# Narrow heads: the larger of two halves' maxima taken on GpSimd, tile by tile, in place of a reduction on VectorE

## The reference

```python
x = layernorm(x + L0_attn(x))   # causal, 16 heads of dimension 8
x = layernorm(x + L0_ffn(x))    # 8 experts, top 2, relu
x = layernorm(x + L1_attn(x))   # causal, low-rank q and k, 16 heads of dimension 8
x = layernorm(x + L1_ffn(x))    # attention, then 8 experts
```

```python
scores = jnp.einsum('bhsk,bhtk->bhst', Q[..., :KPH], K) / math.sqrt(KPH)
attn = jax.nn.softmax(scores, axis=-1)
ao = jnp.einsum('bhst,bhtv->bhsv', attn, V)
```

## Time and profile before

| | us |
|---|---|
| median of 3 runs | 1165.69 |
| the profiled execution, its own time | 1166.3 |
| its span, first to last instruction | 1164.6 |
| TensorE (PE) busy | 1077.7 (93%) |
| VectorE (DVE) busy | 883.9 (76%) |
| ScalarE (ACT) busy | 764.9 (66%) |
| GpSimd (POOL) busy | 305.0 (26%) |
| reductions L1027, 768 in all | 495.5 |

### The profile page before, as it was taken

How to read it: one execution, slowest core, us unless ns; L and a number is a source line. 1 busy time by engine, 2 the same in 40 slices (tenths; PEclk the granted TensorE clock), 3 DMA queues, 4 the chain that set the end, 5 groups by cost and what they waited for, 6 DMA issues and landing times. The chain is left out here.

```text
span 1164.6 us, 24392 instructions
## 1 busy us (share of the span) xinstructions
PE 1077.7 (93%) x8338; PEld 569.1 (49%) x8338; DVE 883.9 (76%) x2563; ACT 764.9 (66%) x1527; POOL 305.0 (26%) x843
## 2 busy tenths in 40 slices
PE   8999999989999988999999998898889898899997
PEld 5465665656767655666655532221122221137775
DVE  6999989882433497889978899799999899804435
ACT  4576776766444446777776677888888688875443
POOL 4234433231115225433346211230110100100001
PEclk9899999999999999999999999999999999999999
DMA  7355431100001601344222221002111000000000
GB/s 200 75 121 156 104 84 33 43 23 2 1 1 38 157 22 33 96 106 103 66 75 56 55 38 25 18 18 45 26 36 38 11 18 13 6 1 1 10 10 19
DMA packets 39563, 57.62 MB, mean 49 GB/s; under 512 B 9408, under 2 KB 14992, under 8 KB 39056
## 3 DMA queue, kind: packets, MB, share of 16 engines
q1 hardware_dynamic: 39440, 56.06, 19.6%
HBM read 30.81 MB, written 24.64 MB: 48 GB/s over the span
## 5 line engine op out<-in xcount | busy, mean ns | idle before, releaser
L911 ACT ACTIVATE probs<-bank 128x512 f32<-128x512 f32 x1088 | 575.9, 601 | 214.8 <-PE bank L1346 213.6
L1027 DVE TENSOR_REDUCE tile_max<-bank 128x1 f32<-128x512 f32 x768 | 495.5, 683 | 55.6 <-PE bank L1332 53.2
L1332 PE MATMUL bank<-qk 125*128 125x512 bf16 (+1 forms) x1280 | 387.2, 356 | 54.9 <-DVE tile_max L1027 41.3
L1346 PE MATMUL bank<-qk 128*128 128x128 bf16 (+1 forms) x1664 | 384.6, 309 | 5.9 <-ACT probs L911 5.5
L1375 PE MATMUL bank<-probs,v_head 128*32 128x512 f32 (+3 forms) x3328 | 304.1, 454 | 0.1
L1332 PEld LDWEIGHTS bank<-qk 125*128 125x128 bf16 (+1 forms) x1280 | 105.4, 96 | 333.1 <-DVE tile_max L1027 225.4
L1023 DVE CUSTOM_DVE_ANT_0 bank<-bank,future 128x512 f32<-128x512 f32 (+3 forms) x512 | 243.5, 506 | 22.2 <-PE bank L1332 22.1
L1187 DVE SCALAR_TENSOR_TENSOR acc<-bank,gate,acc 128x128 f32<-128x128 f32 x248 | 69.7, 343 | 158.4 <-PE bank L1501 158.4
L1346 PEld LDWEIGHTS bank<-qk 128*128 128x128 bf16 (+1 forms) x1664 | 138.2, 97 | 68.1 <-ACT probs L911 22.0
L1375 PEld LDWEIGHTS bank<-probs,v_head 128*32 128x32 f32 x3328 | 139.7, 109 | 53.4 <-issue 30.5
L931 ACT ACTIVATE probs<-bank,sb_b 128x512 f32<-128x512 f32 x128 | 81.0, 684 | 123.1 <-PE bank L1489 123.1
(11 more groups left out here) (148 smaller groups left out, 648.9 us busy)
## 6 DMA issues: line engine op xcount, KB each, us to landing
qk<-qk_parts SPq DMA_DIRECT2D x160, 144.0 KB
qk_parts<-q_parts SPq DMA_DIRECT2D x48, 192.0 KB, 2.4
qk_parts<-k_parts SPq DMA_DIRECT2D x48, 192.0 KB, 2.9
qk_parts<-q_parts SPq DMA_DIRECT2D x24, 96.0 KB, 2.3
qk_parts<-k_parts SPq DMA_DIRECT2D x24, 96.0 KB, 2.9
sb_w<-in_w SPq DMA_DIRECT2D x8, 256.0 KB, 3.7
sb_w<-in_w SPq DMA_DIRECT2D x2, 1024.0 KB, 5.9
qk<-neg_rows SPq DMA_DIRECT2D x96, 6.0 KB
```

The lines of the kernel that those rows point to most:

```text
L911: nc.scalar.activation(probs[:, hd.probs_place(c), :], S2[i % len(S2)][:], ACT.Exp, scale=hd.a.scale).then_inc(sem("probs"), 1)
L1027: ins = nc.vector.tensor_reduce(largest, s1[:, at:at + P * count], AX.X, ALU.max)
L1332: ins = mm(s1[:, at:at + P * count], qk[hd.query_rows, hd.place, 0, P * t:P * (t + 1)], qk[hd.query_rows, hd.place, 1, P * k0:P * (k0 + co ...
L1346: ins = mm(s2[:, at:at + P * count], qk[hd.key_rows, hd.place, 1, P * j:P * (j + 1)], qk[hd.key_rows, hd.place, 0, P * q0:P * (q0 + count) ...
```

## The change

For the narrow heads alone, the seventeenth instruction on VectorE (L1033, with the wait for its own last reduction) goes. GpSimd waits for the last reduction of the head itself (`max_taken`), and before its four steps runs eight instructions, one for each query tile: the larger of the tile's two columns, times -1, written to one column of `neg_max`. Each has one column as its input, the other as a scalar read from SBUF, and a constant. The eight don't wait for each other; the last one is waited for before the first cast. Where VectorE reuses a slot whose last tenant was a narrow head, it waits for the four steps of that head (`neg_parts`) in place of `neg_max`. Causal heads stay as they are.

```diff
@@ split_max, on GpSimd
                 ge(pool, "neg_ps", g - RING + 1)
-                pool.wait_ge(sem("neg_max"), g + 1)
+                if HEADS[g].a.causal:
+                    pool.wait_ge(sem("neg_max"), g + 1)
+                else:
+                    pool.wait_ge(sem("max_taken"), CHUNKS[g + 1])
+                    for t in range(TB):
+                        ins = nc.gpsimd.tensor_scalar(neg_max[:, slot, t:t + 1], tile_max[:, slot, t, 0:1],
+                                                      tile_max[:, slot, t, 1:2], -1.0, ALU.max, ALU.mult)
+                    link(ins)
                 nc.gpsimd.tensor_copy(neg_parts[:, slot, 0, :], whole_m).then_inc(sem("neg_parts"), 1)
@@ find_max, on VectorE
                 if c == 0:
-                    ge(dve, "neg_max", g - RING + 1)
+                    if g - RING >= 2 * NH:
+                        dve.wait_ge(sem("neg_parts"), 4 * (g - RING + 1))
+                    else:
+                        ge(dve, "neg_max", g - RING + 1)
...
-                if c == a.chunks - 1:
+                if a.causal and c == a.chunks - 1:
                     dve.wait_ge(sem("max_taken"), CHUNKS[g + 1])
                     ge(dve, "neg_parts", 4 * (g - RING + 1))
                     nc.vector.tensor_reduce(neg_max[:, hd.slot, :], tile_max[:, hd.slot], AX.X, ALU.max,
                                             negate=True).then_inc(sem("neg_max"), 1)
```

## The result

The changed kernel takes 1229.74 us, the median of 4 runs (1227.06 to 1230.61), against 1165.35 before (the median of four; the prediction started from 1165.69, that of the first three). The ratio is 1.0545, with a 95% interval of 1.0523 to 1.0568: slower by 64 us. The profiled execution took 1227.06, its span is 1225.3 us against 1164.6, so the spans differ by a little less, 60.8 us, than the medians.

What follows compares the result with a forecast made beforehand. A ring of waits between TensorE and VectorE, with the transposition inside, sets the narrow heads' pace. Shift less cover, 32.3 us, less 0.6 for VectorE gives +31.7: 1197.4 us from 1165.7, range 1172 to 1232.

Steps and rivals of the forecast that it cites:

- rival (1): The forecast itself: GpSimd starts 0.13 to 0.30 us apart, split 1.0 to 2.3 us later, +15 to +56 us; 64%.
- rival (2): GpSimd's instructions dearer, starts 0.30 to 0.45 us apart, +56 to +94 us, or TensorE's clock falls after waits; 16%.
- VectorE's relief: Removing the seventeenth reduction frees 0.20 us of VectorE a narrow head, mostly becoming idle time; about 0.6 us gained.
- The lateness passes through in full: At TensorE's transposition (L1354 before the change), a late split delays products and next query score; the ring has no slack.
- shift less cover: Each narrow head pays the split's delay (1.53 us) minus its earlier lead over TensorE's transposition (mostly 0.31 to 0.56).
- I take p = 0.20 and d = 0.25: GpSimd's eight new instructions: spacing p between starts and duration d of the last, in us; shift 1.53 us.
- estimate from the read command: About 102 cycles, 85 ns, per non-overlapping GpSimd read, added to p and d: shift 2.21 us, +53 us.
- the sum: Shift less cover over the narrow heads, 32.3 us, less 0.6 for VectorE: +31.7 us.
- the rest of the span would keep its length: Sign of being right: outside the narrow heads the span stays the same length.
- What would show it: Signs: cast about 1.5 us later, TensorE waiting about 1.1 us in some 30 heads, four-head period near 46.5.
- signs of being wrong: TensorE waits at the transposition in only 2 heads, VectorE's period grows less than the wait, or narrow heads show half-clock stretches.
- a ring of waits: Narrow heads: TensorE's scores wait for banks VectorE's reductions free, and reductions for scores; about 2.5 us per four chunks.

Runs made afterwards that it cites:

- experiment 5: Changed kernel with the narrow heads' transposition and ScalarE's copy of it one batch later in their engines' orders: 1179.63 us, ratio 1.0116 against the kernel before.
- (3): Changed kernel, its eight GpSimd instructions each waiting only for the two reductions of their own tile: 1171.07 us, ratio 1.0033 against the kernel before.
- experiment 4: Changed kernel plus six TensorE matmuls with unread results before the transposition of each narrow head after the first: 1210.54 us, ratio 1.0368 against the kernel before.

## Why the prediction was right, and where it was short

The forecast was 1197.4 us with 1172 to 1232 as its range; 1229.7 lies near the upper end. Its main case had the direction and the mechanism, but about half of the size: +64 lies above the +15 to +56 of rival (1), the forecast itself, and in rival (2), dearer instructions or the clock, to which 16% were given. That the range holds it, by 2 us, is in part luck: the range took in a share of (2), which names both causes but has a price for dearer instructions only, and 18 of the 64 us were the clock.

- **VectorE's relief is worth nothing: right.** 0.6 us was forecast for the stage; the removal alone moved it by 0.35 (the medians differ by 2.4; the rest isn't explained). The busy share of 40.69 in 41.88 was no sign of a bound, the 0.17 us of idle time behind one reduction was.
- **The lateness passes through in full: right.** With the measured spacing the rule, shift less cover, gives 7 x 0.256 + 0.286 - 0.12 = 1.96 us of shift and about 45 us for the 32 heads, less 0.6; the part without the clock was 43.4. In steady heads it gives 6.0 in four, and 5.8 were found. Four and two instructions cost 16 where the rule gave 20, and 4 for 5, and more cover (experiment 5) or an earlier start (3) took most of the loss away, to +12 and +4.
- **The price of the instruction: too low.** The step that failed is "I take p = 0.20 and d = 0.25". It was 0.256 and 0.286: with constants one column starts every 0.17 us, a little less than the 0.20 taken, and the pointer adds 0.084. Seven spacings and 30 heads made of 0.06 us some 13 us. The prediction's estimate from the read command in the Trainium skill ("GPSIMD Engine Reference", Performance pitfalls for Q7 kernels), which it left out of the sum, gave +53. Its 0.085 on top of the measured 0.17 is the measured 0.256.
- **The clock: seen, and put in the wrong place.** The dear rival had waits "of 2 us or more" as its condition; here the clock fell behind waits of 1.36 to 2.23 us, all but one under 2, in some heads and not in others. The sum had nothing for it; about 18 us went to it, 7 in the narrow stage and 11 behind it, where I had written that the rest of the span would keep its length. With the late split at 43.4 where 31.7 was forecast (11.7 more) and the 1.0 us that the part ahead was shorter, that is the whole distance from 31.7 to 60.8.
- **What would show it.** The eight rows, the cast about 2 us later, TensorE's wait at the transposition in nearly all heads, and VectorE's idle time before the reduction (1.46) are there as listed; the period is 47.7, not 46.5, and TensorE's wait 1.5 us and not 1.1. But one of the listed signs of being wrong came as well, the half-clock stretches in the narrow heads, and the rest of the span did not keep its length.

## What to carry to other kernels

A nearly full engine isn't the bound if a ring of waits runs through it: look for the short idle time in front of its instructions once a batch, and what stands inside the ring. Work that is moved to an idle engine is free only while it is shorter than the time between its input and the turn of the instruction that wants it; past that point each tenth is paid in full, in every round. Price many small instructions by the spacing of starts of the very form, with its pointer, because the number is multiplied. And look at TensorE's granted clock behind the new waits: here they cost 18 us on top of their own length, part of it in a stretch that the edit didn't touch.

## What the runs showed of the hardware

- On GpSimd a one-column TENSOR_SCALAR lasts 0.213 us with constants and 0.286 with one scalar from SBUF; starts are 0.172 and 0.256 us apart.
- The granted clock fell to 1.2 GHz for stretches of 3.4 us eleven times in the narrow stage of the changed kernel (one of them 6.8), where the kernel before had two, and once for 30.7 us, from 1067.6 to 1098.3. One of the short ones, the long one, and the wait of TensorE in whose last tenths the long one began:

```profile
722.90:726.30 3.40, 3.40 (x20) 0.58 (x16) 2.23 (x8) 2.06 (x4) 0.00 (x0) 0.50 0.43 63
1067.60:1098.30 30.70, 30.55 (x103) 5.18 (x104) 0.00 (x0) 15.59 (x31) 0.09 (x1) 0.50 0.00 0
...
1067.75 0.28 PE L1365 MATMUL bank<-ident,neg_parts 128*24 128x128 bf16 x1 [1.82 <-POOL neg_parts L734]
1067.76 1.98 PE L1386 MATMUL bank<-probs,v_head 128*32 128x512 f32 x8
```

TensorE was busy in all of the stretch that followed (35.95 of 36.0 us) and still stayed at 1.2 GHz for 30.6 of it. The last long wait before ten of the eleven short stretches was that at the transposition, 1.36 to 2.23 us; the eleventh, of 6.8, stands at a wait of 3.67 us for VectorE, as one does before. Many waits of the same length, as the 1.36 to 1.72 in the steady heads from 829 to 877 and one of 2.19 at 792, had no fall behind them. Why some did is open; that filling the wait removes most of the falls is shown (experiment 4: three stretches are left in its narrow stage).
- Four products with 32 columns of weights each, to four quarters of a bank's rows (eight instructions), take as long as two (four instructions): 1.07 against 1.05 us, and the next matmul starts 1.00 and 0.99 us after the first of them.
